# Spacing the side products of a fused attention kernel: halved projections, a rule against neighbouring units, and zero-valued products at the start

## The chip, the cores and the metric

One core of a Trainium2 chip runs the program. The metric is the device time of one execution in microseconds (us); the time of a kernel is the median of its runs.

## The reference, cut to what matters

Two layers over x of 4 x 1024 x 128 (float32), 16 heads of width 8, each sublayer followed by a residual sum and a layer norm without weights:

```
x = LN(x + attn0(x))   # q, k scaled to unit length, scores / temperature, full softmax, projection + bias
x = LN(x + ffn0(x))    # rows quantised to int8 with a scale of their own, int8 weights, one 128x128 product
x = LN(x + attn1(x))   # per-head layer norm of q and k, rotary embedding, causal softmax, projection + bias
x = LN(x + ffn1(x))    # down(silu(gate(x)) * up(x)), hidden width 384
```

Almost all of the work is attention: the exponential of every score (half of them in the causal layer), and two products of inner size 8 or of output width 8 for each score.

## The kernel before, in words

**Passes and slots.** The 4096 rows are 8 chunks of 512 (`CHUNKS`, line 48, gives the order in which the 16 pairs of layer and chunk are worked). A pass is one group of 4 heads of one chunk in one layer (64 passes, line 50); two passes share one accumulator bank. A step (line 89) is one tile of 128 keys against 512 queries for 4 heads; in the causal layer tiles are put together so that all steps have about the same width. There are 400 steps, and the program is a list of 400 slots, one for each step. In slot s TensorE issues the scores of the coming step as two groups k = 2s+3 and 2s+4 (`scores`, line 970: four products of 32 x 512 by two heads each), and the sums of step s-1 (`sums`, line 996: 8 products with the values, whose extra column of ones gives the softmax denominators). ScalarE takes two exponentials of 128 x 1024 for each step (line 826), 800 in all. Scores lie in three double banks of PSUM, so the scores of group k wait for the exponential of group k-3 (line 984). GpSimd cuts the causal corner out of the probabilities (line 734) and places the values (line 702).

**Units.** All other work is cut into units (lines 109 to 124): `qkv`, `qkT` (turns of q and k), `xqT`, `ffn`, `normT`, `gate`, `up`, `down` and `proj` on TensorE, each filling the one bank `SIDE` and read by VectorE before the next fill (`stage`, line 933; `read`, line 1358), and steps of layer norms, row norms and rotary embedding on VectorE. A job is the chain of units of one chunk: `prep` (before layer 0), `mid` (between the layers, through ffn0) and `last` (ffn1). The projection of a chunk, `proj`, isn't part of a job: it has a fixed slot, three behind the last step of the chunk's fourth pass (line 258), and is 16 calls of the product in four tiles of 128 rows (line 943), then one VectorE sum of 128 x 512 into `x_all` (line 1367).

**The planner.** `side_order` (line 176) writes down once, before the program is built, which units stand in which slot. Jobs are taken by their due slot; `after` is the first slot of a job. A table of costs (lines 146 to 152) keeps a running estimate of when TensorE, ScalarE and VectorE are free. In each slot at most one TensorE unit is placed (`done`), the first live job whose unit fits (`fits`, line 223); what VectorE units fit follow. Slots get one of three orders of TensorE's work: sums behind both score groups and ahead of the unit (the plain order), sums behind the unit (`front`), or sums between the two score groups (`between`, line 241). The list of the kernel before holds 202 TensorE units in 202 slots; 158 of them stand before slot 340, and the last 60 slots hold 44. Nothing in it keeps a unit from standing in the slot behind another unit's.

**Queues.** SP's queue carries the loads of q and k rows (`load_rows`, line 574), the stores of their parts (`send_parts`, line 550) and the output, in the order of a list sorted by the planner's slots (line 640).

**The start.** Before the first scores TensorE turns q and k of the first two chunks. `keep_warm` (line 1043) issues products of a tile of zeros, `warm`, whose result is overwritten later; `WARM` (line 522) counts them at four places. `FIRST_KEYS` (line 170) are three units of the second chunk that stand in slots 0 and 1: the turn of k in slot 0, and in slot 1 the scaling of q (VectorE) and the turn of q.

**The end.** Behind slot 400 `end` (lines 888 and 1301) runs the projection and ffn1 of the last chunk, one step after another.

Of the kernel before, what the change touches and what calls it, by code (L numbers as in the profile page):

```python
# [145 lines left out]
PE_US = {"qkT": 0.6, "normT": 0.6, "qkv": 0.9, "proj": 1.15, "xqT": 0.4, "ffn": 0.4, "gate": 0.7, "up": 0.7, "down": 0.95}  # L146
READ_US = {"qkT": 1.5, "normT": 0.65, "qkv": 0.6, "proj": 0.75, "xqT": 0.45, "ffn": 1.2, "gate": 0.75, "up": 1.5, "down": 0.35}
# [28 lines left out]
def side_order():  # L176
# [10 lines left out]
    for c in range(NCH):  # L187
        after = LAST_STEP[passes_of(0, c)[-1]] + 4
        jobs.append(dict(name="mid", c=c, after=after, due=min(first_slot(passes_of(1, c)[0]) - 4, after + 28)))
    for c in range(NCH - 1):  # L190
        after = LAST_STEP[passes_of(1, c)[-1]] + 4
        jobs.append(dict(name="last", c=c, after=after, due=min(after + 26, NS - 6)))
# [6 lines left out]
    out[1] += FIRST_KEYS[1:]  # L199
    turns = [LAST_STEP[p] + 1 for p in range(1, NP, 2)]  # L200
    pe = act = dve = bank = turned = 0.0
    scores_at = [0.0, 0.0]
    for s in range(NS + 1):
# [31 lines left out]
        project = [p for p in range(1, NP, 2) if PASSES[p][3] == GB - 1 and LAST_STEP[p] + 3 == s]  # L235
        if pending or not ends_pair(s - 1) and s <= NS - FREE and (
                dve < pe - 0.1 if project else any(fits(j, pe - AHEAD) for j in live)):
            front.add(s)
        else:
            one = max(free, act - act_time(s) / 2 if s < NS else 0.0) + 0.45 + cost  # L240
            if s < NS - 1 and max(one, act) + 0.45 < sums - GAIN:
                between.add(s)
                sums = one
                pe = max(one, act) + 0.45
                scores_at[-1] = pe + 0.05
            else:
                pe = sums
        done = False
        late = []
        for p in range(1, NP, 2):  # L250
            layer, b, qh, g = PASSES[p]
            if LAST_STEP[p] + 1 == s:
                out[s].append((None, p, "dve", "turn", p))
# [4 lines left out]
            if g == GB - 1 and LAST_STEP[p] + 3 == s:  # L258
                out[s].append((None, p, "pe", "proj", p))
                pe = max(pe, bank) + PE_US["proj"]  # L260
                dve = bank = max(dve, pe + 0.15) + READ_US["proj"]
                done = True
        for j in live:
# [4 lines left out]
            if not fits(j, pe + (SLACK if s < NS - END else LATE)):  # L268
                continue
# [30 lines left out]
SLACK, LATE, OVER, TURN_BY, END, FREE, AHEAD, GAIN = 0.2, 1.5, 1.6, 1.6, 60, 3, 0.0, -0.2  # L300
# [89 lines left out]
def program(nc, a, ctx):  # L390
# [131 lines left out]
    WARM = (10, 4, 0, 22)  # L522
# [340 lines left out]
    def _(pe):  # L863
# [69 lines left out]
        def stage(name, c, what, k):  # L933
# [4 lines left out]
            if what == "proj":  # L938
                layer, b, qh, g = PASSES[k]
                if k == GB - 1:  # L940
                    pe.wait_ge(late_consts, 1)
                pe.wait_ge(attn_ready, k // GB + 1)
                for t in range(TC):
# [124 lines left out]
        def steps(shifted):  # L1068
# [10 lines left out]
            for s in range(NS + 1):  # L1079
                for k in (2 * s + 3, 2 * s + 4):  # L1080
                    if k < 2 * NS:
                        scores(k, shifted)
                    if k % 2 and s in BETWEEN:
                        sums(s - 1)
                if s and s not in FRONT and s not in BETWEEN:
                    sums(s - 1)
# [15 lines left out]
    def _(dve):  # L1102
# [255 lines left out]
        def read(name, c, what, k):  # L1358
# [4 lines left out]
            if what == "proj":  # L1363
                layer, b, qh, g = PASSES[k]
                dve.wait_ge(bias_added, k // GB + 1)
                x = x_all[:, b * NH2 + qh, :, :]
                tt(x, side_t, x, ALU.add).then_inc(side_read, 1)  # L1367
# [176 lines left out]
```

## Time and profile before

| what | value |
|---|---|
| median of 3 runs | 831.9 us (831.88 to 832.3) |
| the profiled execution, its own time | 833.45 us |
| its span, first to last instruction | 831.4 us |
| mean granted TensorE clock | 0.993 of full speed |
| VectorE busy | 540.3 us (65%) |
| GpSimd busy | 169.9 us (20%) |
| first exponential starts | 20.24 us |
| last exponential starts | 805.6 us |

How to read it: the span is 2.05 us shorter than the execution's own time, and that execution is 1.55 us above the median. The stretch from the first to the last exponential is the 400 slots; 20 us before it are the head, 25 us behind it the end. Busy time of TensorE counts matmuls from issue to a modelled end, and these overlap, so it says when TensorE had work in flight and not how much more it could take.

### The profile page before, as it was taken

How to read it: one execution, taken by the hardware profiler on the slowest of the kernel's cores; microseconds unless marked ns; L12 is line 12 of the kernel's file. 1: busy time of each engine (PE TensorE's matmuls, PEld its weight loads, DVE VectorE, ACT ScalarE, POOL GpSimd, SP SyncE). 2: the span in 40 equal slices, each digit the busy share in tenths (PEclk: the TensorE clock that was granted, in tenths of full speed). 3: DMA queues.
4: the chain of work that ended last, by engine and by line, in shares of the span. 5: the costliest groups of instructions: out<-in, count | busy, mean ns of one | idle time of the engine just before them, and what ended most of it. 6: DMA issues, size and time to landing. Idle time of an engine off the chain costs nothing.

```text
span 831.4 us, 18912 instructions
## 1 busy us (share of the span) xinstructions
PE 803.6 (97%) x7457; PEld 295.6 (36%) x7457; DVE 540.3 (65%) x1426; ACT 772.3 (93%) x869; POOL 169.9 (20%) x370
## 2 busy tenths in 40 slices
PE   8899999999999999999999999999999999999996
PEld 4223332333333433343333433343333343443444
DVE  4265666868867787876663677675754267785656
ACT  4899999999999999999999999999999999898972
POOL 3110000100000601033000611023200354362220
PEclk9899999999999999999999999999999999999999
DMA  5765414242602631362130421321231231071000
GB/s 144 248 225 190 177 40 146 83 141 76 242 27 88 231 140 39 99 232 78 59 133 26 150 81 39 140 90 45 72 130 51 81 110 51 27 240 53 15 14 15
DMA packets 48556, 88.74 MB, mean 107 GB/s; under 512 B 5200, under 2 KB 14544, under 8 KB 48464
## 3 DMA queue, kind: packets, MB, share of 16 engines
q1 hardware_dynamic: 47696, 85.95, 30.4%
q8 instruction: 61, 1.00, 0.5%
q0 software_dynamic: 288, 1.05, 0.4%
q10 hardware_dynamic: 480, 0.48, 0.2%
q14 instruction: 31, 0.25, 0.1%
HBM read 50.50 MB, written 35.65 MB: 104 GB/s over the span
## 4 chain that ended last, share of the span: by engine, by line
PE 75%; ACT 13%; DVE 7%; issue 3%; DMA 0%; ACTq 0%; DVEq 0%
PE ps L1011 37%; PE ps L989 21%; ACT probs L826 13%; PE ps L879 9%; PE ps L868 3%; PE ps L964 3%; DVE th L1421 1%; DVE hT L1422 1%; PE ps L873 1%; PE ps L1045 1%; PE ps L1053 0%; DVE sums_t L1249 0%; DVE gate_sb L1416 0%; DVE mid_part L1411 0%; DVE mid_part L1412 0%
## 5 line engine op out<-in xcount | busy, mean ns | idle before, releaser
L826 ACT ACTIVATE probs<-ps 128x1024 f32<-128x1024 f32 x800 | 749.3, 1057 | 31.0 <-PE ps L989 21.2
L1011 PE MATMUL ps<-probs,v_st 128*32 128x512 f32 (+3 forms) x3584 | 428.1, 560 | 3.2 <-issue 2.4
L989 PE MATMUL ps<-q_st,k_st 32*128 32x512 f32 (+3 forms) x1792 | 266.3, 460 | 7.8 <-ACT probs L826 7.2
L989 PEld LDWEIGHTS ps<-q_st,k_st 32*128 32x128 f32 x1792 | 120.1, 182 | 288.0 <-ACT probs L826 221.7
L734 POOL TENSOR_SCALAR_AFFINE_SELECT probs<-probs 128x256 f32<-128x256 f32 x256 | 103.8, 428 | 144.7 <-ACT probs L826 143.0
L1011 PEld LDWEIGHTS ps<-probs,v_st 128*32 128x32 f32 x3584 | 78.7, 108 | 110.4 <-issue 74.2
L702 POOL COPY v_st<-v_all 128x256 f32<-128x256 f32 (+1 forms) x65 | 29.1, 456 | 343.2 <-PE ps L1011 334.9
L1249 DVE STREAM_TRANSPOSE sums_t<-ps 128x512 f32<-128x512 f32 x32 | 22.9, 716 | 45.3 <-PE ps L1011 44.7
L1390 DVE COPY mid_qkv<-ps 128x384 f32<-128x384 f32 x32 | 17.8, 557 | 35.8 <-PE ps L879 34.8
L964 PE MATMUL ps<-yTp,w_hid 128*128 128x512 f32 x84 | 31.2, 453 | 4.1 <-DVE gate_sb L1416 2.5
L1390 DVE COPY prep_qkv<-ps 128x384 f32<-128x384 f32 x24 | 13.4, 558 | 27.1 <-PE ps L879 26.4
L879 PE MATMUL ps<-w_cols,yT 128*32 128x384 f32 x256 | 26.7, 489 | 0.0
L1426 DVE TENSOR_TENSOR last_y<-ps,last_y 128x128 f32<-128x128 f32 x24 | 7.0, 292 | 28.8 <-PE ps L879 28.4
L1421 DVE SCALAR_TENSOR_TENSOR th<-th,gate_sb 128x512 f32<-128x512 f32 x21 | 14.8, 707 | 16.6 <-PE ps L964 16.2
L879 PE MATMUL ps<-w_down,hT 128*32 128x128 f32 x672 | 23.8, 275 | 1.1 <-DVE last_y L1426 0.6
L724 POOL TENSOR_TENSOR x_all<-x_all,vecs 128x512 f32<-128x512 f32 x16 | 23.3, 1459 | 1.1 <-DMA x_all<-in_x 1.1
L1367 DVE TENSOR_TENSOR x_all<-ps,x_all 128x512 f32<-128x512 f32 x15 | 10.4, 691 | 20.3 <-PE ps L879 12.4
L964 PEld LDWEIGHTS ps<-yTp,w_hid 128*128 128x128 f32 x84 | 12.6, 189 | 29.5 <-issue 9.3
L1416 DVE COPY gate_sb<-ps 128x512 f32<-128x512 f32 x21 | 14.5, 692 | 12.7 <-PE ps L964 12.4
L879 PEld LDWEIGHTS ps<-w_down,hT 128*32 128x32 f32 x672 | 17.9, 110 | 13.2 <-issue 7.4
L697 POOL COPY v_all<-prep_qkv 128x512 f32<-128x512 f32 x6 | 3.7, 614 | 85.7 <-DVEq L1393 85.7
L879 PE MATMUL ps<-w_cols,xT 128*32 128x384 f32 x192 | 20.1, 490 | 0.4 <-DVE hT L1422 0.2
(190 smaller groups left out, 641.3 us busy)
## 6 DMA issues: line engine op xcount, KB each, us to landing
k_st<-parts_scratch SPq DMA_DIRECT2D x46, 512.0 KB, 3.6
parts_scratch<-mid_part SPq DMA_DIRECT2D x34, 512.0 KB, 4.4
q_st<-parts_scratch SPq DMA_DIRECT2D x62, 256.0 KB, 3.9
parts_scratch<-prep_part SPq DMA_DIRECT2D x28, 512.0 KB, 4.8
k_st<-parts_scratch SPq DMA_DIRECT2D x17, 256.0 KB, 2.9
xT<-in_xT SPq DMA_DIRECT2D x8, 256.0 KB, 4.4
x_all<-in_x SPq DMA_DIRECT2D x8, 256.0 KB, 5.3
out<-yo SPq DMA_DIRECT2D x7, 256.0 KB, 2.3
```

The costliest lines, as they stand in the source:

```text
L702: return g_.tensor_copy(v_st[:, p % VB, t, :, p % 2 * SR:p % 2 * SR + D], v_all[:, layer, b % 2, t, g * GH * D:(g + 1) * GH * D] .rearrang ...
L724: g_.tensor_tensor(x_all[:, c, :, :], x_all[:, c, :, :], bc(vecs[:, 3 * layer, :].unsqueeze(1), [P, TC, C]), ALU.add).then_inc(bias_added, 1)
L734: op = g_.affine_select(out=block_, in_=block_, compare_op=ALU.is_ge, fill=0.0, base=0, pattern=[[0, 2], [1, P]], channel_multiplier=-1)
L826: nc.scalar.activation(probs[:, k % PS, :, 0:w], slot(k)[:, :, 0:w], ACT.Exp).then_inc(probs_ready, 1)
L868: last_ = tp(dst[:, t * P:(t + 1) * P], src(t), idn[:])
L879: last_ = mm(dst[row, :], src[:, row], w, start=first, stop=last)
L964: last_ = mm(side, w_hid[:, 0 if what == "gate" else 1, k * P:(k + 1) * P], yTp[:, n, :], start=(n == 0), stop=(n == PARTS - 1))
L989: last_ = mm(slot(k)[:, e, at:at + n], k_st[row, p % KB, kt * P:(kt + 1) * P], q_st[row, p % KB, lo:HALF], start=True, stop=not shifted)
L1011: last_ = mm(acc[HR * h:HR * (h + 1), lo:HALF], v_st[:, p % VB, kt, h, :], probs[:, (2 * s + h // 2) % PS, h % 2, at:at + n], start=FIRST[ ...
L1249: v.transpose(sums_t[:], acc).then_inc(sums_turned, 1)
L1390: v.tensor_copy(job[name]["qkv"][:, k, :], side[:, 0:3 * C]).then_inc(side_read, 1)
L1421: chain[lane(name, c)].link(stt(out=th[:, k % 2, :], in0=th[:, k % 2, :], scalar=1.0, in1=gate_sb[:, k % 2, :], op0=ALU.add, op1=ALU.mult))
```

## The change

- The projection of a chunk becomes two units of two tiles each, in the third and in the fourth slot behind the chunk, each with a VectorE sum of 128 x 256. The jobs that follow it start one slot later (`+ 5` for `+ 4`), and the table of costs has the new sizes.
- Up to slot 340 a TensorE unit is not placed when the slot before it holds one, as long as the job still reaches its due slot by the estimate `slots_left`: one slot for each TensorE unit left and 0.6 for each VectorE unit left.
- In slots 0 and 1, behind each of the score groups 3 to 6, two products of the zero tile go into the accumulator bank (which the first sums overwrite).
- The turn of q of the second chunk moves from slot 1 to slot 2, and the order with sums between the score groups is used only from slot 7 on.

```
@@ -143,8 +143,8 @@
 
 
 
-PE_US = {"qkT": 0.6, "normT": 0.6, "qkv": 0.9, "proj": 1.15, "xqT": 0.4, "ffn": 0.4, "gate": 0.7, "up": 0.7, "down": 0.95}
-READ_US = {"qkT": 1.5, "normT": 0.65, "qkv": 0.6, "proj": 0.75, "xqT": 0.45, "ffn": 1.2, "gate": 0.75, "up": 1.5, "down": 0.35}
+PE_US = {"qkT": 0.6, "normT": 0.6, "qkv": 0.9, "proj": 0.5, "xqT": 0.4, "ffn": 0.4, "gate": 0.7, "up": 0.7, "down": 0.95}
+READ_US = {"qkT": 1.5, "normT": 0.65, "qkv": 0.6, "proj": 0.45, "xqT": 0.45, "ffn": 1.2, "gate": 0.75, "up": 1.5, "down": 0.35}
 DVE_US = {"ln_stats": 0.9, "ln_aggr": 0.8, "ln_out": 1.2, "ln_out_x": 1.2, "ln_out_y": 1.2, "amax": 1.2, "quant": 1.0,
           "round": 1.0, "ffn_bias": 0.75, "add": 0.75, "square": 1.7, "norms": 1.3, "scale": 1.3,
           "rope0": 1.3, "rope1": 1.5, "rope2": 1.3, "rope3": 1.3, "weights": 2.8, "centre": 1.5, "rot": 2.0,
@@ -185,10 +185,10 @@
         after = first_slot(passes_of(0, c // NH2 * NH2 - NH2 - 1)[-1]) + 3 if c >= 2 * NH2 else BRANCHED
         jobs.append(dict(name="prep", c=c, after=after, due=first_slot(passes_of(0, c // NH2 * NH2)[0]) - 4))
     for c in range(NCH):
-        after = LAST_STEP[passes_of(0, c)[-1]] + 4
+        after = LAST_STEP[passes_of(0, c)[-1]] + 5
         jobs.append(dict(name="mid", c=c, after=after, due=min(first_slot(passes_of(1, c)[0]) - 4, after + 28)))
     for c in range(NCH - 1):
-        after = LAST_STEP[passes_of(1, c)[-1]] + 4
+        after = LAST_STEP[passes_of(1, c)[-1]] + 5
         jobs.append(dict(name="last", c=c, after=after, due=min(after + 26, NS - 6)))
     jobs.append(dict(name="consts", c=0, after=BRANCHED, due=16))
     for j in jobs:
@@ -196,8 +196,14 @@
     jobs.sort(key=lambda j: (j["due"], j["c"]))
     out, front, between = [[] for _ in range(NS + 1)], set(), set()
     out[0] += FIRST_KEYS[:1]
-    out[1] += FIRST_KEYS[1:]
+    out[1] += FIRST_KEYS[1:2]
+    out[2] += FIRST_KEYS[2:]
     turns = [LAST_STEP[p] + 1 for p in range(1, NP, 2)]
+
+    def slots_left(j):
+
+        return sum(REST if e == "pe" else 0.6 for e, what, k in UNITS[j["name"]][j["n"]:])
+
     pe = act = dve = bank = turned = 0.0
     scores_at = [0.0, 0.0]
     for s in range(NS + 1):
@@ -232,13 +238,13 @@
                     return False
             return True
 
-        project = [p for p in range(1, NP, 2) if PASSES[p][3] == GB - 1 and LAST_STEP[p] + 3 == s]
+        project = [p for p in range(1, NP, 2) if PASSES[p][3] == GB - 1 and 0 <= s - LAST_STEP[p] - 3 < 2]
         if pending or not ends_pair(s - 1) and s <= NS - FREE and (
                 dve < pe - 0.1 if project else any(fits(j, pe - AHEAD) for j in live)):
             front.add(s)
         else:
             one = max(free, act - act_time(s) / 2 if s < NS else 0.0) + 0.45 + cost
-            if s < NS - 1 and max(one, act) + 0.45 < sums - GAIN:
+            if BRANCHED <= s < NS - 1 and max(one, act) + 0.45 < sums - GAIN:
                 between.add(s)
                 sums = one
                 pe = max(one, act) + 0.45
@@ -255,8 +261,8 @@
                 turned = dve - 0.9
                 if g == GB - 1 and p < NP - 1:
                     late.append((None, p, "dve", "yT", p))
-            if g == GB - 1 and LAST_STEP[p] + 3 == s:
-                out[s].append((None, p, "pe", "proj", p))
+            if g == GB - 1 and 0 <= s - LAST_STEP[p] - 3 < 2:
+                out[s].append((None, p, "pe", "proj", s - LAST_STEP[p] - 3))
                 pe = max(pe, bank) + PE_US["proj"]
                 dve = bank = max(dve, pe + 0.15) + READ_US["proj"]
                 done = True
@@ -266,6 +272,8 @@
             name, c = j["name"], j["c"]
             e, what, k = UNITS[name][j["n"]]
             if not fits(j, pe + (SLACK if s < NS - END else LATE)):
+                continue
+            if s < NS - END and any(x[2] == "pe" for x in out[s - 1]) and s + slots_left(j) < j["due"]:
                 continue
             out[s].append((name, c, e, what, k))
             j["n"] += 1
@@ -297,7 +305,7 @@
 
 
 
-SLACK, LATE, OVER, TURN_BY, END, FREE, AHEAD, GAIN = 0.2, 1.5, 1.6, 1.6, 60, 3, 0.0, -0.2
+SLACK, LATE, OVER, TURN_BY, END, FREE, AHEAD, GAIN, REST = 0.2, 1.5, 1.6, 1.6, 60, 3, 0.0, -0.2, 1.0
 SIDE_ORDER, JOBS, FRONT, BETWEEN = side_order()
 
 LEFT = [(j["name"], j["c"], *u) for j in JOBS for u in j["left"]]
@@ -519,7 +527,7 @@
     shift_out, shift_in = sem("shift_out"), sem("shift_in")
 
     POOL_CONSTS = 11
-    WARM = (10, 4, 0, 22)
+    WARM = (10, 4, 0, 22, 7)
     NLATE = 9
     layer_job = ("prep", "mid")
     buffers = lambda name, c: job["mid" if (name, c) == ("prep", 1) else name]
@@ -936,11 +944,11 @@
             if fill:
                 pe.wait_ge(side_read, fill)
             if what == "proj":
-                layer, b, qh, g = PASSES[k]
-                if k == GB - 1:
+                layer, b, qh, g = PASSES[c]
+                if c == GB - 1:
                     pe.wait_ge(late_consts, 1)
-                pe.wait_ge(attn_ready, k // GB + 1)
-                for t in range(TC):
+                pe.wait_ge(attn_ready, c // GB + 1)
+                for t in range(2 * k, 2 * k + 2):
                     last_ = quarters(side[:, t * P:(t + 1) * P], attn[:, t * P:(t + 1) * P], w_out[:, layer, :])
             elif what == "normT":
                 pe.wait_ge(norm_ready[lane(name, c)], norm_number(name, c))
@@ -1082,6 +1090,8 @@
                         scores(k, shifted)
                     if k % 2 and s in BETWEEN:
                         sums(s - 1)
+                    if k < WARM[4]:
+                        keep_warm(2, ACC)
                 if s and s not in FRONT and s not in BETWEEN:
                     sums(s - 1)
                 for name, c, e, what, k in SIDE_ORDER[s]:
@@ -1361,10 +1371,10 @@
             got = lambda: dve.wait_ge(side_read, fill + 1)
             dve.wait_ge(side_filled, fill + 1)
             if what == "proj":
-                layer, b, qh, g = PASSES[k]
-                dve.wait_ge(bias_added, k // GB + 1)
-                x = x_all[:, b * NH2 + qh, :, :]
-                tt(x, side_t, x, ALU.add).then_inc(side_read, 1)
+                layer, b, qh, g = PASSES[c]
+                dve.wait_ge(bias_added, c // GB + 1)
+                x = x_all[:, b * NH2 + qh, tiles(k), :]
+                tt(x, side_t[:, tiles(k), :], x, ALU.add).then_inc(side_read, 1)
                 got()
             elif what == "normT" and name == "last":
                 ch = chain[lane(name, c)]
```

## Rows read from the trace of the kernel before

**Rows 1.** Page, part 1: busy time, share of the span, instructions

```profile
PE 803.6 (97%) x7457; PEld 295.6 (36%) x7457; DVE 540.3 (65%) x1426; ACT 772.3 (93%) x869; POOL 169.9 (20%) x370
```

**Rows 2.** Page, part 5, exponentials: busy, mean ns, idle before them and its releaser

```profile
L826 ACT ACTIVATE probs<-ps 128x1024 f32<-128x1024 f32 x800 | 749.3, 1057 | 31.0 <-PE ps L989 21.2
```

**Rows 3.** Timeline of ScalarE: start, duration, group, count, idle before it

```profile
20.24 6.52 ACT L826 ACTIVATE probs<-ps 128x1024 f32<-128x1024 f32 x7 [3.98 <-PE ps L989]
28.53 1.02 ACT L826 ACTIVATE probs<-ps 128x1024 f32<-128x1024 f32 x1 [1.77 <-PE ps L989]
30.95 110.32 ACT L826 ACTIVATE probs<-ps 128x1024 f32<-128x1024 f32 x117 [1.40 <-PE ps L989]
...
757.69 1.02 ACT L826 ACTIVATE probs<-ps 128x1024 f32<-128x1024 f32 x1 [2.16 <-PE ps L989]
```

**Rows 4.** Timeline of ScalarE in three windows: dense units, alternating units, no units

```profile
304.07 13.43 ACT L826 ACTIVATE probs<-ps 128x1024 f32<-128x1024 f32 x13
...
601.62 13.90 ACT L826 ACTIVATE probs<-ps 128x1024 f32<-128x1024 f32 x15 [0.36 <-PE ps L989]
...
639.00 21.19 ACT L826 ACTIVATE probs<-ps 128x1024 f32<-128x1024 f32 x23 [0.16 <-PE ps L989]
```

**Rows 5.** Timeline of TensorE around a whole projection (L879 with w_out)

```profile
89.53 0.59 PE L989 MATMUL ps<-q_st,k_st 32*128 32x512 f32 x4
90.05 1.06 PE L1011 MATMUL ps<-probs,v_st 128*32 128x512 f32 x8
90.93 1.06 PE L879 MATMUL ps<-w_out,attn 128*32 128x128 f32 x32
91.92 0.51 PE L989 MATMUL ps<-q_st,k_st 32*128 32x512 f32 x4
...
93.35 0.68 PE L989 MATMUL ps<-q_st,k_st 32*128 32x512 f32 x4
```

**Rows 6.** Timeline of VectorE: sums of a whole and of a half projection

```profile
92.06 0.69 DVE L1367 TENSOR_TENSOR x_all<-ps,x_all 128x512 f32<-128x512 f32 x1 [2.03 <-PE ps L879]
...
811.20 0.42 DVE L1308 TENSOR_TENSOR x_all<-ps,x_all 128x256 f32<-128x256 f32 x1 [0.61 <-PE ps L896]
```

**Rows 7.** Timeline of TensorE at the start, and one turn later (60.81)

```profile
1.27 4.45 PE L1045 MATMUL ps<-warm 128*128 128x512 bf16 x10 [1.27 <-DVE warm L1110]
...
14.27 4.91 PE L1045 MATMUL ps<-warm 128*128 128x512 bf16 x22
...
24.07 0.79 PE L989 MATMUL ps<-q_st,k_st 32*128 32x512 f32 x2 [0.42 <-ACT probs L826]
24.79 1.94 PE L1011 MATMUL ps<-probs,v_st 128*32 128x512 f32 x8
26.65 1.12 PE L868 MATMUL ps<-ident,mid_qk 128*128 128x128 f32 x4
...
60.81 0.66 PE L868 MATMUL ps<-ident,prep_qk 128*128 128x128 f32 x4
```

**Rows 8.** Table by stretch: length; busy PE, PEld, DVE, ACT, POOL; granted clock, DMA share, GB/s

```profile
22.00:23.00 1.00, 0.50 (x2) 0.18 (x2) 0.85 (x2) 1.00 (x3) 0.16 (x1) 1.00 0.38 90
...
24.00:25.00 1.00, 0.94 (x6) 0.48 (x10) 0.00 (x0) 1.00 (x3) 1.00 (x5) 0.50 0.84 315
...
31.00:32.00 1.00, 1.00 (x10) 0.18 (x2) 0.00 (x0) 1.00 (x2) 0.00 (x0) 1.00 1.01 377
...
754.00:757.50 3.50, 3.50 (x14) 0.86 (x14) 1.41 (x2) 1.54 (x2) 0.54 (x2) 0.51 0.02 5
```

**Rows 9.** Timeline of SP, a load of q for pass 2; page, part 6, such loads

```profile
40.68 0.43 SPq L572 DMA_DIRECT2D q_st<-parts_scratch  x1
...
q_st<-parts_scratch SPq DMA_DIRECT2D x62, 256.0 KB, 3.9
```

**Rows 10.** Timeline of TensorE in slot 375 and of VectorE behind slot 397

```profile
753.96 1.13 PE L964 MATMUL ps<-yTp,w_hid 128*128 128x512 f32 x2 [1.31 <-DVE gate_sb L1416]
...
806.96 1.12 DVE L1188 TENSOR_SCALAR yo<-mid_y,mid_tok 128x128 f32<-128x128 f32 x4
```

More of the change, by code:

```diff
@@ L142, in ends_pair @@
     return STEPS[s][5] and STEPS[s][0] % 2 == 1
-PE_US = {"qkT": 0.6, "normT": 0.6, "qkv": 0.9, "proj": 1.15, "xqT": 0.4, "ffn": 0.4, "gate": 0.7, "up": 0.7, "down": 0.95}
-READ_US = {"qkT": 1.5, "normT": 0.65, "qkv": 0.6, "proj": 0.75, "xqT": 0.45, "ffn": 1.2, "gate": 0.75, "up": 1.5, "down": 0.35}
+PE_US = {"qkT": 0.6, "normT": 0.6, "qkv": 0.9, "proj": 0.5, "xqT": 0.4, "ffn": 0.4, "gate": 0.7, "up": 0.7, "down": 0.95}
+READ_US = {"qkT": 1.5, "normT": 0.65, "qkv": 0.6, "proj": 0.45, "xqT": 0.45, "ffn": 1.2, "gate": 0.75, "up": 1.5, "down": 0.35}
 DVE_US = {"ln_stats": 0.9, "ln_aggr": 0.8, "ln_out": 1.2, "ln_out_x": 1.2, "ln_out_y": 1.2, "amax": 1.2, "quant": 1.0,
@@ L198, in side_order, with slots_left @@
     out[0] += FIRST_KEYS[:1]
-    out[1] += FIRST_KEYS[1:]
+    out[1] += FIRST_KEYS[1:2]
+    out[2] += FIRST_KEYS[2:]
     turns = [LAST_STEP[p] + 1 for p in range(1, NP, 2)]
+    def slots_left(j):
+        return sum(REST if e == "pe" else 0.6 for e, what, k in UNITS[j["name"]][j["n"]:])
     pe = act = dve = bank = turned = 0.0
@@ L233, in fits @@
             return True
-        project = [p for p in range(1, NP, 2) if PASSES[p][3] == GB - 1 and LAST_STEP[p] + 3 == s]
+        project = [p for p in range(1, NP, 2) if PASSES[p][3] == GB - 1 and 0 <= s - LAST_STEP[p] - 3 < 2]
         if pending or not ends_pair(s - 1) and s <= NS - FREE and (
@@ L240, in side_order @@
             one = max(free, act - act_time(s) / 2 if s < NS else 0.0) + 0.45 + cost
-            if s < NS - 1 and max(one, act) + 0.45 < sums - GAIN:
+            if BRANCHED <= s < NS - 1 and max(one, act) + 0.45 < sums - GAIN:
                 between.add(s)
@@ L257, in side_order @@
                     late.append((None, p, "dve", "yT", p))
-            if g == GB - 1 and LAST_STEP[p] + 3 == s:
-                out[s].append((None, p, "pe", "proj", p))
+            if g == GB - 1 and 0 <= s - LAST_STEP[p] - 3 < 2:
+                out[s].append((None, p, "pe", "proj", s - LAST_STEP[p] - 3))
                 pe = max(pe, bank) + PE_US["proj"]
@@ L268, in side_order @@
             if not fits(j, pe + (SLACK if s < NS - END else LATE)):
+                continue
+            if s < NS - END and any(x[2] == "pe" for x in out[s - 1]) and s + slots_left(j) < j["due"]:
                 continue
@@ L521, in program @@
     POOL_CONSTS = 11
[L522 removed]
+    WARM = (10, 4, 0, 22, 7)
     NLATE = 9
@@ L938, in stage @@
             if what == "proj":
-                layer, b, qh, g = PASSES[k]
-                if k == GB - 1:
+                layer, b, qh, g = PASSES[c]
+                if c == GB - 1:
                     pe.wait_ge(late_consts, 1)
-                pe.wait_ge(attn_ready, k // GB + 1)
-                for t in range(TC):
+                pe.wait_ge(attn_ready, c // GB + 1)
+                for t in range(2 * k, 2 * k + 2):
                     last_ = quarters(side[:, t * P:(t + 1) * P], attn[:, t * P:(t + 1) * P], w_out[:, layer, :])
@@ L1363, in read @@
             if what == "proj":
[L1364 to L1367, printed above, removed]
+                layer, b, qh, g = PASSES[c]
+                dve.wait_ge(bias_added, c // GB + 1)
+                x = x_all[:, b * NH2 + qh, tiles(k), :]
+                tt(x, side_t[:, tiles(k), :], x, ALU.add).then_inc(side_read, 1)
                 got()
```

8 lines of the change are left out of this document (5 added, 3 removed).

## The prediction

> **What bounds the kernel now.** I read the page's busy shares first. TensorE is at 97%, ScalarE at 93% [rows 1], so either could be the bound, and the share is a mean over stages. The exponentials decide: 800 of them, with 31.0 us of idle time ahead of them, most of it waiting for scores [rows 2]. ScalarE's timeline gives their pace. Where slots hold no unit, 23 exponentials take 21.19 us, and since the last one is seen for 1.02 us that is (21.19 - 1.02)/22 = 0.917 us each, 1.83 us for a slot [rows 4]; I take this as ScalarE's own pace. Where every slot holds a unit, it is (13.43 - 1.02)/12 = 1.034, or 2.07 us for a slot [rows 4]. So ScalarE is the bound where units are rare and TensorE where they stand in a row, 0.24 us worse for each slot. The third row is the one to remember: units at slots 300, 302, 304, 306 and 307, and the exponentials still come every (13.90 - 1.02)/14 = 0.920 us [rows 4]. A unit with an empty slot behind it costs almost nothing, because TensorE needs only 93.35 - 91.92 = 1.43 us for an empty slot [rows 5], 0.40 less than ScalarE, and catches up.
>
> All 800 at 0.917 us would take 734 us; the first start and the last lie 785 us apart. The 21 tanh that ScalarE also runs are a small part of the 51 us between; the rest is lost, and three things in this change reach for it.
>
> **1. The start.** Seven exponentials run on time, then ScalarE waits 1.77 and 1.40 us [rows 3]: 3.17 us in all. Ahead of that TensorE was busy for half of the stretch from 22 to 23 us, and from 24 us the granted clock is 0.50, that is 1.2 GHz, until it is back at 1.00 from 31 us [rows 8]. The first sums take 1.94 us and the turn of q 1.12 [rows 7], where at full clock the same work takes 1.06 [rows 5] and 0.66 [rows 7]. The change fills the gaps between the score groups 3 to 6 with pairs of zero products. Do such products hold the clock? The first ten took 4.45/10 = 0.445 us each, the later 22 only 4.91/22 = 0.223 [rows 7], so zero-valued products run at the full rate, with nothing else in between. A pair takes 0.45 us and the gaps are 0.42 [rows 7], covered by the exponentials, of which there are always two ahead. With the clock held, group 6 issues at 24.07, its pair ends at 24.95, the sums at 26.0, and group 7 is done by 26.5; the eighth exponential is due at 20.24 + 7 x 0.917 = 26.66, so no wait. The turn of q, now in slot 2, then sits between the sums of step 1 and group 9: 26.5 + 0.5 + 1.06 + 0.66 = 28.7, against 28.5 due. I take 3.17 - 0.2 = **-2.9 us**. Bounds: -3.17, and +1.7 if the clock falls all the same and half of the eight products (0.445 each at the low clock) lie on the path.
>
> What could be late next: everything at the start is wanted 3 us earlier. The tightest are the q rows of pass 2, issued at 40.68 and landing 3.9 us later, at 44.6 [rows 9]; group 32 would then be issued at about 20.24 + 29 x 0.917 = 46.8. Two microseconds remain. The stores that these loads wait for stand behind others in SP's queue and not behind the turn of q, which by the sum above ends no later than before.
>
> **2. The halved projections.** A whole one makes its slot 91.92 - 89.53 = 2.39 us long on TensorE [rows 5], 0.56 over ScalarE's pace. Half adds 0.48 to the empty 1.43: 1.91, 0.08 over. Twice 0.08 for 0.56 would save 0.40; if each half cost as much as a unit in a row (0.24), it would save 0.08. Slack of the empty slots around already absorbs some of the 0.56, so I take 0.25, for 15 projections **-3.75 us** (bounds -6.0 and -1.2). VectorE reads two halves of 0.42 for one of 0.69 [rows 6]; it is 65% busy [rows 1], and its next readers wait for TensorE. Starting the jobs one slot later costs nothing up to slot 340: the rows of a `mid` chunk are first needed tens of slots behind its due slot.
>
> **3. The spaced units.** From the planner's list of the kernel before I count 94 units before slot 340 that stand directly behind another: 35 second in a run, 59 further back. At 0.24 us for those further back, and half of it for the second (which the slack of the slot before partly pays), that is 59 x 0.24 + 35 x 0.12 = 18.4 us. How many remain? Between the slots 7, 57, 132, 232 and 340 there were 20, 39, 52 and 45 units in 50, 75, 100 and 108 slots; with the second halves 21, 42, 56 and 49. The two middle stretches hold more than every second slot can take, and u units in n slots leave at least 2u - n - 1 neighbours: 8 and 11. Jobs close to their due slot may also run on. A `mid` job has 28 slots and an estimate of 9 + 0.6 x 24 = 23.4, so it can afford about 5 of its 6 gaps; a `last` job has 26 for 17; `prep` has room throughout. I guess 40 neighbours, 30 of them second: 30 x 0.12 + 10 x 0.24 = 6.0 us, and 1.0 us more for the many new lone units. **18.4 - 7.0 = -11.4 us** (bounds: -16 with only the 19 that must remain, 0 if the rule seldom bites).
>
> **4. The last 60 slots.** The rule is off there; the jobs start one slot later. In slot 375 a gate waited 1.31 us for VectorE [rows 10], the clock went to 0.51 at 754 us [rows 8], and ScalarE lost 2.16 us [rows 3]. A plan shifted by a slot may miss this (-3) or meet it elsewhere; VectorE's last piece of the seventh chunk, 1.12 us at 806.96 [rows 10], may slide into the closing chain (+2). I take 0.
>
> **Sum:** -2.9 - 3.75 - 11.4 + 0 = -18.0. The profiled execution took 833.45, so it would be 815.4; the median of the runs is 1.55 lower, and 831.9 - 18.0 = **813.9, say 814 us**.
>
> **The rivals.**
> - **The clock falls at the start anyway.** The zero products come only from group 3 on, and the turn of k lies in the same stretch. Then part 1 is between 0 and +1.7: 814 + 2.9 + 1 = **818**. For it: one fall there is on record; against it: the 22 at full rate. The Trainium skill ("TensorE: Matmul & The Clock Gate", Part 4) says that a transpose does not count as activity as a matmul does; by that rule the moved turn of q would help the clock nowhere, and the time would be this rival's. No row here shows what a turn alone does to the clock.
> - **TensorE is full.** If 97% [rows 1] meant that it has nothing to give, order would not matter and only the start would gain: 831.9 - 2.9 = **829**. Against it: the alternating stretch [rows 4]. The Trainium skill ("Trainium Kernel Development and Optimization", Best Practices) warns against judging TensorE by matmul busy time and points to the share of weight loading; that is 36% here [rows 1], which leaves room, and the trace's 1.43 us agrees.
> - **Crowding, slower.** Put-off units gather before their due slots, where three jobs run at once (slots 132 to 232), and the halves take 15 more slots. Parts 1 and 2 give 6.65 us, which 6.65/0.24 = 28 more neighbours would eat: from 122 of them on (94 before) the change loses. With 150 it would be 831.9 - 6.65 + 56 x 0.24 = **839**. For it: the rule puts off without looking at what else falls due; against it: due slots are staggered and the count of units hardly grows.
> - **All of it.** 19 neighbours, full gain of the halves, and no fall of the clock at 754: 831.9 - 2.9 - 6 - 13 - 3 = **807**.
>
> **How the numbers follow.** The forecast (809 to 820) has 0.52, the fallen clock 0.17, all of it 0.12, a full TensorE 0.09, crowding 0.08, something late at the start or the end 0.02. The range must leave out no more than 0.2: from 806 (all of it) to 826 (the fallen clock with a smaller part 3), leaving out a full TensorE and crowding. A difference of 0.2%, 1.7 us, is about what a measurement of this kernel can tell. Faster by more has the first four cases, less a little for a full TensorE with nothing gained at the start: 0.88; the same 0.04; slower 0.08.
>
> **What would show it.** Right: a granted clock of 1.00 from 22 to 31 us, sums of 1.06 us there, and exponentials in one row from 20.24 on; slots with half a projection at about 1.9 us; the idle time ahead of the exponentials down from 31.0 to under 20 us; the stretch from 289 to 330 us, dense now, at less than 2 us a slot. Wrong: a row of 0.50 in the clock before 31 us; the dense pace of 1.034 over as many exponentials as now; idle exponentials waiting for DMA near 47 us, or the last one later than 800 us.

## The result, and the profile after

The change takes 827.48 us, median of three runs (826.92 to 827.58), against 831.9: ratio 0.9937, 95% interval 0.9922 to 0.9952. By the medians that is 4.4 us faster where 18 were forecast, 1.5 us above the range. The profiled execution took 827.58 us, with a span of 825.4 (831.4 before).

The page of the kernel after, part 1 (as [rows 1]), and from part 5 the exponentials (as [rows 2]) and the projections:

```profile
PE 793.8 (96%) x7457; PEld 294.5 (36%) x7457; DVE 539.2 (65%) x1437; ACT 770.9 (93%) x873; POOL 172.4 (21%) x370
...
L834 ACT ACTIVATE probs<-ps 128x1024 f32<-128x1024 f32 x800 | 747.1, 1058 | 27.2 <-PE ps L997 22.0
...
L887 PE MATMUL ps<-w_out,attn 128*32 128x128 f32 x480 | 18.8, 274 | 5.0 <-DVE attn L1266 5.0
```

The same group of projections in the kernel before, from its groups of TensorE by shape:

```profile
L879 PE MATMUL ps<-w_out,attn 128*32 128x128 f32 x480 | 16.0, 274 | 0.0
```

The busy shares hardly move. The idle time ahead of the exponentials falls from 31.0 to 27.2 us, of which the start alone should have given 3. And TensorE now waits 5.0 us ahead of the projections, for VectorE's `attn`; before, that group waited for nothing.

**The start** did what it should. Timeline of TensorE (as [rows 7]), then of ScalarE (as [rows 3]), then the table by stretch (as [rows 8]), all of the kernel after:

```profile
21.44 0.60 PE L1053 MATMUL ps<-warm 128*128 128x512 bf16 x2
...
24.87 1.07 PE L1019 MATMUL ps<-probs,v_st 128*32 128x512 f32 x8
...
27.30 0.66 PE L876 MATMUL ps<-ident,mid_qk 128*128 128x128 f32 x4
```

```profile
19.93 126.43 ACT L834 ACTIVATE probs<-ps 128x1024 f32<-128x1024 f32 x137 [4.01 <-PE ps L997]
```

```profile
22.00:23.00 1.00, 1.00 (x7) 0.33 (x6) 0.85 (x2) 1.00 (x2) 0.46 (x1) 1.00 0.42 115
24.00:25.00 1.00, 1.00 (x8) 0.33 (x12) 0.00 (x0) 1.00 (x2) 1.00 (x6) 1.00 0.99 365
28.00:29.00 1.00, 1.00 (x12) 0.23 (x12) 0.96 (x2) 0.93 (x2) 0.00 (x0) 1.00 0.73 260
```

The granted clock stays at 1.00 (2.4 GHz), the first sums take 1.07 us and the turn of q 0.66, and 137 exponentials run in one row where 7 did.

**The slots.** To compare the rest I took the starts of all 800 exponentials from the trace and computed how much longer than 1.81 us each slot is (the median slot without a unit takes 1.807), with 0.52 taken out for each tanh. A unit in slot s shows at the exponentials of step s+2. Over slots 4 to 337, count, mean and sum in us (the last column is an experiment told below):

| the slot holds | before | after | early turn |
|---|---|---|---|
| a projection, whole or half | 12, 0.405, 4.9 | 24, 0.238, 5.7 | 24, 0.019, 0.5 |
| no unit | 179, 0.012, 2.1 | 167, 0.007, 1.2 | 167, 0.007, 1.2 |
| a unit, none in the slot ahead | 49, 0.072, 3.5 | 91, 0.108, 9.9 | 91, 0.112, 10.2 |
| the second unit in a row | 35, 0.164, 5.7 | 20, 0.163, 3.3 | 20, 0.162, 3.2 |
| one further back in a row | 59, 0.257, 15.1 | 32, 0.238, 7.6 | 32, 0.235, 7.5 |

The neighbours give back 10.0 us, and the lone units (those with none in the slot ahead), of which there are now 91, take 6.4 of it. The projections, halved, cost more than whole.

The same count, parted by the kind of unit, shows part of why a lone unit now costs more on average. Without the five dearest, which are told of further below, the lone `ffn` and `xqT` of the kernel after cost 0.00 us (8 of them), the turns of q and k 0.06 (20), `qkv` 0.10 (31). In a row, `ffn` and `xqT` still cost 0.00 and `qkv` 0.27. TensorE works 0.85 us on a `qkv`, 0.66 on a turn and 0.40 on an `xqT`. Of the 42 new lone units 28 are `qkv`.

Why they do is seen at one of them. Timeline of all engines of the kernel after, slots 96 to 98 (start, duration, what ran, the idle time before it and its releaser):

```profile
202.70 0.72 DVE L1259 STREAM_TRANSPOSE sums_t<-ps 128x512 f32<-128x512 f32 x1 [0.53 <-PE ps L1019]
...
203.84 0.43 DVE L1263 TENSOR_TENSOR heads_t<-sums_t,rd 128x256 f32<-128x256 f32 x1
204.30 0.56 DVE L1400 COPY prep_qkv<-ps 128x384 f32<-128x384 f32 x1
...
204.77 1.22 DVE L1250 TENSOR_TENSOR mid_qk<-mid_qk,rot 128x1024 f32<-128x1024 f32 x1
...
206.13 0.71 DVE L1266 STREAM_TRANSPOSE attn<-heads_t 128x512 f32<-128x512 f32 x1
...
206.99 0.64 PE L887 MATMUL ps<-w_out,attn 128*32 128x128 f32 x16 [0.74 <-DVE attn L1266]
...
208.10 2.90 ACT L834 ACTIVATE probs<-ps 128x1024 f32<-128x1024 f32 x3 [0.66 <-PE ps L997]
```

Read it down VectorE. The chunk's sums are turned and divided by 204.27; the next step, the turn into `attn`, takes 0.71 us. But the planner lists it (`yT`) at the end of the slot, behind that slot's units: a copy of `qkv` and a rotary step run first, 1.8 us. TensorE reaches the first half projection, finds no `attn`, and stands 0.74 us; ScalarE then stands 0.66. By the planner's lists, 8 of the 13 chunk ends before slot 340 have a unit or a piece between `turn` and `yT` after the change, 4 before it: the rule puts units off into those slots. Waits of TensorE in the kernel after (in total, how many, the longest):

```profile
PE ps L887 <- DVE attn L1266: 5.0, 7, 1.2
...
PE ps L887 <- DVE hT L1432: 1.4, 2, 1.1
PE ps L876 <- DVEq L1305: 1.4, 1, 1.4
...
PE ps L876 <- DVE mid_qkv L1400: 1.2, 1, 1.2
```

**The end.** Slots 340 to 399 cost 15.7 us over pace, 16.5 before. But from the end of the last exponential to the end of the span it is 26.7 us, 24.7 before. The planner now leaves two `down` units and five VectorE pieces of the seventh chunk behind slot 400. Timelines of TensorE, VectorE and ScalarE at the end of the kernel after:

```profile
803.69 1.52 PE L887 MATMUL ps<-w_down,hT 128*32 128x128 f32 x48
```

```profile
815.23 0.16 DVE L383 TENSOR_SCALAR mid_tok<-mid_tok 128x4 int32<-128x4 int32 x1
...
816.80 0.16 DVE L1324 SCALAR_TENSOR_TENSOR mid_tok<-mid_tok 128x4 f32<-128x4 f32 x1
816.91 0.42 DVE L1352 TENSOR_TENSOR last_y<-ps,last_y 128x256 f32<-128x256 f32 x1
...
822.03 0.60 DVE L1362 TENSOR_SCALAR yo<-last_y,last_tok 128x128 f32<-128x128 f32 x2 [0.94 <-DMA out<-yo]
```

```profile
817.00 1.65 ACT L860 ACTIVATE yo<-mid_y,mid_tok 128x128 f32<-128x128 f32 x4 [4.37 <-DVE mid_tok L1324]
```

Nine small VectorE operations for the seventh chunk's norm stand from 815.23 to 816.96 just ahead of the sum that closes the last chunk, and near the end VectorE waits 0.94 us for a store.

**The account:** start -3.3 us, slots 4 to 339 -3.5, slots 340 to 399 -0.8, end +2.0, first exponential 0.3 earlier: -5.9, and the spans differ by 6.0. (The first exponential lies anywhere from 19.2 to 20.5 us in the profiles of this study; differences of single profiles are good to about a microsecond for that alone. The profiled execution of before was also 1.55 above its median, so that by medians 4.4 are left.)

### The profile page after: what moved, and what is told of

It reads as the page before. It is cut to its first block, busy times and chain, and to the rows that moved or that the text cites. A ratio compares the mean times of both kernels' runs of the same rounds, so it can differ in the third digit from the quotient of the medians.

```text
span 825.4 us, 18983 instructions
## 1 busy us (share of the span) xinstructions
PE 793.8 (96%) x7457; PEld 294.5 (36%) x7457; DVE 539.2 (65%) x1437; ACT 770.9 (93%) x873; POOL 172.4 (21%) x370
## 4 chain that ended last, share of the span: by engine, by line
PE 65%; DVE 15%; ACT 13%; issue 5%; DMA 1%; ACTq 0%; DVEq 0%
PE ps L1019 32%; PE ps L997 18%; ACT probs L834 13%; PE ps L887 7%; PE ps L972 3%; PE ps L876 3%; DVE th L1431 1%; DVE sums_t L1259 1%; DVE hT L1432 1%; DVE mid_y L1220 1%; PE ps L1053 1%; DVE attn L1266 1%; DVE heads_t L1263 1%; DVE mid_part L1421 1%; DVE mid_part L1422 1%
## 5 line engine op out<-in xcount | busy, mean ns | idle before, releaser
L834 ACT ACTIVATE probs<-ps 128x1024 f32<-128x1024 f32 x800 | 747.1, 1058 | 27.2 <-PE ps L997 22.0
L997 PE MATMUL ps<-q_st,k_st 32*128 32x512 f32 (+3 forms) x1792 | 258.2, 459 | 2.8 <-ACT probs L834 2.3
L742 POOL TENSOR_SCALAR_AFFINE_SELECT probs<-probs 128x256 f32<-128x256 f32 x256 | 106.0, 436 | 143.3 <-ACT probs L834 141.8
L710 POOL COPY v_st<-v_all 128x256 f32<-128x256 f32 (+1 forms) x65 | 31.0, 485 | 327.7 <-PE ps L1019 319.7
L1377 DVE TENSOR_TENSOR x_all<-ps,x_all 128x256 f32<-128x256 f32 x30 | 12.7, 425 | 27.9 <-PE ps L887 27.4
L887 PE MATMUL ps<-w_cols,yT 128*32 128x384 f32 x256 | 26.9, 491 | 0.4 <-DVE mid_qkv L1400 0.4
L705 POOL COPY v_all<-mid_qkv 128x512 f32<-128x512 f32 x9 | 5.5, 612 | 97.1 <-DVEq L1403 92.0
L887 PE MATMUL ps<-w_out,attn 128*32 128x128 f32 x480 | 18.8, 274 | 5.0 <-DVE attn L1266 5.0
```

The source lines that it names most:

```text
L710: return g_.tensor_copy(v_st[:, p % VB, t, :, p % 2 * SR:p % 2 * SR + D], v_all[:, layer, b % 2, t, g * GH * D:(g + 1) * GH * D] .rearrang ...
L742: op = g_.affine_select(out=block_, in_=block_, compare_op=ALU.is_ge, fill=0.0, base=0, pattern=[[0, 2], [1, P]], channel_multiplier=-1)
L834: nc.scalar.activation(probs[:, k % PS, :, 0:w], slot(k)[:, :, 0:w], ACT.Exp).then_inc(probs_ready, 1)
L887: last_ = mm(dst[row, :], src[:, row], w, start=first, stop=last)
L997: last_ = mm(slot(k)[:, e, at:at + n], k_st[row, p % KB, kt * P:(kt + 1) * P], q_st[row, p % KB, lo:HALF], start=True, stop=not shifted)
```

## The experiments

Each was timed against the kernel before on the same chip. The short names: the **rule** is the one against neighbours, **early turn** is the edit that lists `yT` early. In the texts on record e2 is the change without the rule, e3 early turn and e10 the run with 44 slots.

### The start part alone, on the kernel before

```
-    out[1] += FIRST_KEYS[1:]
+    out[1] += FIRST_KEYS[1:2]
+    out[2] += FIRST_KEYS[2:]
...
-            if s < NS - 1 and max(one, act) + 0.45 < sums - GAIN:
+            if BRANCHED <= s < NS - 1 and max(one, act) + 0.45 < sums - GAIN:
...
+                    if k < WARM[4]:
+                        keep_warm(2, ACC)
```

> The kernel before with the start of the change alone (zero products behind score groups 3 to 6, turn of q in slot 2, no sums between the groups ahead of slot 7). Theory A (the clock kept at 1.00 gives back the 3.2 us of waits): 831.9 - 3.2 = 828.7, between 828 and 829.5, and the idle time ahead of the exponentials down by 3. Theory B (the start only moves the waits to the loads behind it): 831 to 832. Under A the rule and the halves together gave only about 1 us of the 4.4.

Measured 829.52 us, ratio 0.9961 (0.9947 to 0.9976): 2.5 us. Slots 0 to 3 lose 0.17 us in place of 3.47; slots 4 to 339 lose 31.7, for 31.4 before. The start part is worth about what it was forecast at, and the halves, the rule and the end together only some 2 us. A second fall of the clock shows in this kernel too. TensorE waits for `gate` twice, at 702 and at 752 us (1.2 and 1.3 us), as in the kernel before. In the profile of this run the clock falls to 0.50 behind the first wait, in that of the kernel before behind the second [rows 8]; the slot behind the wait loses 2.2 or 2.3 us with the fall and 0.7 without it, so the fall costs 1.5.

### The change without the zero-valued products, and with the turn of q back in slot 1

```
-                    if k < WARM[4]:
-                        keep_warm(2, ACC)
```

> The changed kernel without the zero products in the first two slots; all else stays. Theory A (they keep the clock, and the clock was the start's whole loss): a granted clock of 0.50 from about 24 us again, sums of 1.94 us, waits of 2 to 3 us ahead of the eighth and later exponentials, 827.5 + 2.5 = 830, between 829.5 and 831. Theory B (moving the turn of q out of slot 1 already avoids the waits): 827 to 828.

```
-    out[1] += FIRST_KEYS[1:2]
-    out[2] += FIRST_KEYS[2:]
+    out[1] += FIRST_KEYS[1:]
```

> The changed kernel with the turn of q back in slot 1; zero products stay. Theory A (at full clock the turn costs at most a few tenths wherever it stands): 827.5 to 828. Theory B (the turn in slot 1 waits for VectorE and holds the scores up): 828.5 to 829.5, with a wait of over 0.5 us ahead of the eighth exponential.

Without the products 829.11 us (0.9961, 0.9947 to 0.9974), 1.6 above the whole change and a little under the range of A; with the turn in slot 1 828.23 (0.995, 0.9935 to 0.9966), 0.75 above, between the two ranges. Both intervals overlap the change's own, so the clock and the profiles have to decide. The mean granted clock is 0.992 in all five executions without the products, and 0.997 to 0.998 in those of the change and with the turn in slot 1 (one at 0.996). Table by stretch and ScalarE's timeline without the products, then ScalarE's timeline with the turn in slot 1:

```profile
22.00:23.00 1.00, 0.50 (x2) 0.18 (x2) 0.85 (x2) 1.00 (x2) 0.01 (x1) 1.00 0.36 90
24.00:25.00 1.00, 0.79 (x6) 0.36 (x10) 0.00 (x0) 1.00 (x3) 1.00 (x5) 0.50 0.68 258
28.00:29.00 1.00, 1.00 (x8) 0.00 (x0) 0.00 (x0) 1.00 (x2) 0.00 (x0) 0.50 0.63 193
```

```profile
27.64 1.94 ACT L834 ACTIVATE probs<-ps 128x1024 f32<-128x1024 f32 x2 [0.73 <-PE ps L997]
31.09 9.27 ACT L834 ACTIVATE probs<-ps 128x1024 f32<-128x1024 f32 x10 [1.52 <-PE ps L997]
```

```profile
26.37 13.87 ACT L833 ACTIVATE probs<-ps 128x1024 f32<-128x1024 f32 x15 [0.54 <-PE ps L996]
```

Without the products the clock falls to 0.50 again and two waits come back, 2.25 us; they sit where [rows 3] had them. With the turn in slot 1 and the products kept there is one wait of 0.54 and no fall. So the products hold the clock, and the moved turn saves about half a microsecond of TensorE's time at a tight place.

### The change without the rule

```
-            if s < NS - END and any(x[2] == "pe" for x in out[s - 1]) and s + slots_left(j) < j["due"]:
-                continue
```

> The changed kernel without the rule against neighbouring units; halves and start stay. By the planner's list the neighbours before slot 340 rise from 64 to 107. Theory A (each neighbour costs 0.2 us, the rule pays for itself): 827.5 + 43 x 0.2 = 836, less some waits for VectorE at chunk ends, so 832 to 836. Theory B (what the rule saves in neighbours it loses in waits for late VectorE pieces and in costs of lone units): 826 to 829.

Measured 831.69 us (0.9996, 0.9987 to 1.0005), just under the range of A: the rule is worth 4.2 us in the change, and the halves with the later jobs, on top of the start, cost 2.2. Half projections cost 0.094 us a slot here, 2.3 in all for 4.9 when whole, but the second halves make 107 neighbours out of 94, the rows further back cost 17.3 us for 15.1, and the end part is 26.9 us. TensorE waits for `attn` 1.9 us, for 5.0 with the rule: that wait needs the rule to grow.

```profile
PE ps L885 <- DVE attn L1264: 1.9, 3, 0.7
```

### Early turn: the same plan, with `yT` listed directly behind `turn`

```
+    for items in out:
+        for x in [x for x in items if x[3] == "yT"]:
+            items.remove(x)
+            items.insert([y[3] for y in items].index("turn") + 1, x)
```

> The changed kernel with the same plan, except that in the slot behind a chunk the turn of the heads (yT) is listed directly behind the turn of the sums, ahead of the units that the rule pushed into that slot. Theory A (the first half of the projection waits 5.0 us in all for this turn, because put-off units stand ahead of it): those waits fall under 1 us, and the time falls by 4 to 5, to 822.5 to 824. Theory B (the waits only move to the reads that now come later): 826.5 to 827.5.

Measured 822.27 us, ratio 0.988 (0.9863 to 0.9896), 5.2 us below the change: the interval lies wholly under the change's. All units stand in the same slots; only VectorE's order within nine of them differs. The same place as above, in the timeline of this kernel:

```profile
203.86 0.42 DVE L1267 TENSOR_TENSOR heads_t<-sums_t,rd 128x256 f32<-128x256 f32 x1
204.32 0.71 DVE L1270 STREAM_TRANSPOSE attn<-heads_t 128x512 f32<-128x512 f32 x1
...
204.95 0.52 DVE L1404 COPY prep_qkv<-ps 128x384 f32<-128x384 f32 x1
...
205.40 1.21 DVE L1254 TENSOR_TENSOR mid_qk<-mid_qk,rot 128x1024 f32<-128x1024 f32 x1
...
206.09 0.62 PE L891 MATMUL ps<-w_out,attn 128*32 128x128 f32 x16
```

The turn comes first, the half projection starts with no wait, 0.9 us earlier, and the copy and the rotary step lose nothing that shows. The waits for `attn` are gone from the list, half projections cost 0.019 us a slot (the table above), and the page has the exponentials at

```profile
L838 ACT ACTIVATE probs<-ps 128x1024 f32<-128x1024 f32 x800 | 746.1, 1064 | 22.8 <-PE ps L1001 18.0
```

This shows the cause of the projections' missing gain.

### Early turn without the rule

The second and the third edit together.

> Run e3 (early turn of the heads, 822.3) without the rule against neighbouring units: neighbours before slot 340 rise from 64 to 107, projections no longer wait. Theory A (a neighbour costs 0.22 and a lone unit 0.11, so the rule is worth about 7 us once the turn is early): 829 to 830.5. Theory B (the rule is worth 4 us whatever stands at the chunk ends, as between e2 and the changed kernel): 826 to 827.

Measured 830.42 us (0.9976, 0.9965 to 0.9986). With the turn early the rule is worth 830.42 - 822.27 = 8.1 us, with the turn late 4.2: some 4 us of what the rule gains were spent at the chunk ends.

### Whole projections, with the rule and the start part

The projection becomes one unit again in its third slot, and the jobs start at `+ 4`; in short

```
-            if g == GB - 1 and 0 <= s - LAST_STEP[p] - 3 < 2:
-                out[s].append((None, p, "pe", "proj", s - LAST_STEP[p] - 3))
+            if g == GB - 1 and (s - LAST_STEP[p] - 3 == 0 or s - LAST_STEP[p] - 3 == 1 and LAST_STEP[p] < 0):
+                half = LAST_STEP[p] < 0
+                out[s].append((None, p, "pe", "proj", s - LAST_STEP[p] - 3 if half else 2))
...
-                for t in range(2 * k, 2 * k + 2):
+                for t in range(4) if k == 2 else range(2 * k, 2 * k + 2):
```

> The changed kernel with whole projections again in the third slot behind a chunk and jobs from the fourth (costs of the table as before); rule and start stay. Neighbours before slot 340 fall to 48, nothing is left for the end. Theory A (halving gave 0.4 for each projection only where the turn was early, and cost neighbours and 1.8 us at the end): 825 to 828. Theory B (halving is worth the 3.75 us of the prediction): 830 to 832.

Measured 827.68 us (0.9948, 0.9934 to 0.9963): the same as the change. As it stands, halving is worth nothing. A whole projection costs 0.595 us here (7.1 in all, with two waits for `attn`), nothing is left behind slot 400, and the end part is back at 24.7 us. Halving gains in the slots (27.9 us over pace in slots 4 to 339, for 30.3 whole) what it loses at the end.

### Early turn, with whole projections and earlier jobs from slot 320 on

The same edit on early turn, with 320 in the place of 0, and `+ 4` for the chunks behind that slot alone.

> Run e3 (822.3) with whole projections and jobs one slot earlier from slot 320 on, so that the last slots hold the plan of the kernel before and nothing is left for the end. Theory A (halves in the full last slots push two down units and five VectorE pieces of the seventh chunk behind the last exponential, where they and the wait for its output lengthen the end from 24.8 to 27.6 us): the end is 24.8 us again, three whole projections cost about 1 us back, 820 to 821.5. Theory B (the end is set by the last chunk's own chain and only seems longer): 822.5 to 823.5.

Measured 822.13 us (0.9876, 0.9861 to 0.9892): no different from early turn. The end part fell as it should, from 27.5 to 24.7 us (the expectation has both 0.1 longer), and slots 340 to 399 took 1.7 of it back (15.4 to 17.1). In the list of TensorE's waits the one for `gate`, which the kernel before had too [rows 10] and early turn had not, is back:

```profile
PE ps L977 <- DVE gate_sb L1432: 3.1, 2, 1.9
```

Behind the longer of the two waits the granted clock is at 0.51 from 743.5 to 747 us.

### Early turn, with the sums ahead of the unit in nearly all slots

Is it the order within a slot that makes a lone unit cost 0.11 us?

```
+    for s in range(BRANCHED, NS - END):
+        if s in front and not (STEPS[s - 1][4] and STEPS[s - 1][0] % 2 == 0):
+            front.discard(s)
```

> Run e3 (822.3) with the same plan, but sums ahead of the unit (plain order) in all slots from 7 to 339 except where a pass begins; e3 had the unit ahead of the sums in most slots with a lone unit, and a lone unit cost 0.11 us there (91 of them, 10.2 us). Theory A (a lone unit costs that because TensorE can save up only about 0.2 us in an empty slot, in any order): 822 to 823. Theory B (the order holds the next scores up behind unit and sums): 3 to 5 us faster, 817.5 to 819.5.

Measured 824.53 us (0.9922, 0.9907 to 0.9937), 2.3 above early turn, slower than either theory had it, with lone units at 0.117. So it isn't that the unit stood ahead of the sums.

### Early turn, with later due slots: 44, 52, and 52 for the early jobs only

More room for the rule. The edit with 44 (42 for `last`), and that of the third of them (the second has 52 and 50 for every chunk), cut to the ends of the lines:

```
-due=min(first_slot(passes_of(1, c)[0]) - 4, after + 28)))
+due=min(first_slot(passes_of(1, c)[0]) - 4, after + 44)))
...
-due=min(first_slot(passes_of(1, c)[0]) - 4, after + 28)))
+due=min(first_slot(passes_of(1, c)[0]) - 4, after + (52 if c < 6 else 28))))
...
-due=min(after + 26, NS - 6)))
+due=min(after + (50 if c <= 3 else 26), NS - 6)))
```

> Run e3 (822.3) with later due slots for the jobs between and behind the layers (after + 44 for + 28, after + 42 for + 26), so that the rule can space more: neighbours before slot 340 fall from 64 to 42. Theory A (a neighbour made lone saves 0.22 - 0.11): 822.3 - 22 x 0.11 = 819.9, between 819 and 821. Theory B (put-off units meet late VectorE pieces and the waits eat it): 822 to 824. Theory C (the 0.23 of the prediction for each): 817.5.

> As run e10, with after + 52 and after + 50: neighbours fall to 30, of which 12 are the second halves of projections. Theory A: 822.3 - 34 x 0.11 = 818.6, between 817.5 and 819.5. Theory B: 822 to 825. Theory C: 814.5.

Measured 832.55 us (1.0008, 0.9999 to 1.0017) with 44, and 828.72 (0.9963, 0.9949 to 0.9976) with 52, both slower than any of the theories. One wait takes the gain away in both, 8.2 and 8.3 us. Waits of TensorE, ScalarE's timeline and the table by stretch with 52:

```profile
PE ps L1001 <- DMA q_st<-parts_scratch: 8.3, 1, 8.3
```

```profile
740.69 1.02 ACT L838 ACTIVATE probs<-ps 128x1024 f32<-128x1024 f32 x1 [7.54 <-PE ps L1001]
743.22 11.12 ACT L838 ACTIVATE probs<-ps 128x1024 f32<-128x1024 f32 x12 [1.50 <-PE ps L1001]
```

```profile
735.00:738.00 3.00, 0.00 (x0) 0.00 (x0) 0.13 (x1) 0.00 (x0) 0.00 (x0) 0.50 0.64 197
738.00:744.00 6.00, 4.20 (x30) 1.37 (x30) 0.00 (x0) 1.81 (x2) 0.40 (x1) 0.50 0.99 339
744.00:748.00 4.00, 3.65 (x48) 1.28 (x40) 1.72 (x4) 4.00 (x6) 1.33 (x4) 1.00 0.55 198
```

The last chunk's turns of q and k moved from slots 363 and 364 to 368 and 369, TensorE waited 8.3 us for the rows of q, and the clock stood at 0.50 around the hole. In slots 4 to 339, though, 34 fewer neighbours (30 for 64) saved 2.8 us, 20.0 for 22.8: 0.08 each. With 44 the 22 fewer saved only 0.6 us, 22.2 for 22.8: 0.03 each. Why so little isn't known. Hence the last run, which leaves the late jobs as they were:

> The early-turn kernel with the later due slots of the run before it, but only for jobs that end before slot 340: `mid` of chunks 0 to 5 due 52 slots behind its start, `last` of chunks 0 to 3 due 50 behind; `mid` of chunks 6 and 7 and the later `last` jobs keep the early-turn kernel's own due slots, so chunk 7's turns of q and k stand in slots 363 and 364 again instead of 368 and 369. Units behind a unit before slot 340: 39 (early turn 64, with all jobs late 30). Theory A: the 8.3 us wait for q_st was the whole harm of the late due slots, and a neighbour that gets room saves about 0.08 us: 25 x 0.08 = 2.0 us under the early-turn kernel's 822.3, so 820.3 us, slots 4 to 339 about 20.8 us over 1.81 each, no wait for q_st over 1 us. Theory B: VectorE's pieces pushed towards the end cost in the last 60 slots what the room saves: 822 to 824 us, slots 340 to 399 over 16.5 us.

Measured 820.72 us (819.3 to 821.57), ratio 0.9853 (0.9834 to 0.9873), the fastest kernel of the study, 11.8 us under the kernel before on that chip. Slots 4 to 339 cost 20.6 us (20.8 was expected), slots 340 to 399 15.8, and the wait for `q_st` is gone. Its interval overlaps that of early turn a little; the slots' 2.2 us agree with the difference. Its page has

```profile
L838 ACT ACTIVATE probs<-ps 128x1024 f32<-128x1024 f32 x800 | 745.1, 1052 | 21.0 <-PE ps L1001 17.7
```

and 123 units without a neighbour ahead still cost 13.9 us: that is what is left to find.

## Why the prediction was right, and where it was wrong

**Part by part.** Of 18.0 us forecast 5.9 came by the spans: the start -3.3 (-2.9 forecast), the halves +0.8 on the 12 projections before slot 340 (-3.75 on 15), the spacing -3.6 (-11.4), the last slots and the end +1.2 (0), and -1.0 in slots without a unit and ahead of the first exponential. The miss lies in the halves, 4.6 us, and in the spacing, 7.8.

**What bounds the kernel: right.** ScalarE where units are rare, TensorE where they stand in rows. The second unit in a row cost 0.164 us (0.12 taken), one further back 0.257 (0.24 taken).

**1. The start: right.** -2.9 forecast, -2.5 by the run of the start alone and -3.3 in the slots. No load was late behind it. The clock did not fall, so the first rival is out. The rule of the Trainium skill cited there ("TensorE: Matmul & The Clock Gate", Part 4, that a transpose does not count as activity as a matmul does) was not put to the test: with the products in place the clock stayed at 1.00 with the turn in either slot.

**2. The halves: the mechanism right, the step that failed is "its next readers wait for TensorE".** A projection gained 0.405 - 2 x 0.019 = 0.37 us when the turn was early (0.25 taken), but in the change the 12 before slot 340 lost 0.8 us together. A slot with a half, 1.91 us in the sum, took 2.05 in the change and 1.83 with the turn early. I costed VectorE's side by its busy share, 65%, and by the sums behind the projection, and never asked what it does ahead of it. An engine with a third of its time free still does its list in order, and 1.8 us of work with room to spare stood ahead of a 0.71 us turn with none. The early-turn run shows it. In the kernel before, the turn stood behind other work at 4 of these 13 places, and no projection waited: the waits came with the plan of the change.

**3. The spacing: the step that failed is the sum for what remains.** The gain on the neighbours was sized well for its count: 20.9 us before (18.4 taken) and 10.9 after. But 64 neighbours remained, 12 of them second halves, where I guessed 40; and the new lone units, which I gave 1.0 us, took 6.4. I had read "costs almost nothing" from one stretch of alternating units [rows 4], at 0.920 us per exponential, and carried it to all. The kernel before had 49 lone units already, at 0.072 us each, and its trace would have shown it ahead of the forecast. In the change a lone unit costs 0.108 us on average. Five of the 91 cost over 0.25 us, 3.2 us together, and four of these, 2.9 us, stand behind waits for VectorE; the other 86 cost 0.077 each. That cost goes with the kind of unit, and most of the new lone units are of the dear kind, `qkv`; why a `qkv` with an empty slot ahead still costs 0.10 us no run shows. A neighbour that is given room therefore saves not 0.24 but 0.08 or 0.09, by the run with 52 and the last run, and 0.03 by the run with 44. The guess of 40 fell because the due slots and not the rule set how many remain: with 52 slots for the job there are 30.

**4. The end: 0 taken, +2.0 measured, -0.8 in the last 60 slots.** The +2 was named, but for one VectorE piece that slides; it was two units and five pieces. With whole projections and the jobs one slot earlier nothing is left over, and the end part is 24.7 us; which of the two does it was not tried. The -3 was half there: both waits for `gate` (2.5 us) and the fall of the clock behind them (1.5) are gone, but other waits for VectorE, 1.4 us for `hT` and 1.2 for `mid_qkv` in the list above among them, took most of it back.

**The rivals.** A full TensorE gave 829 and the result lies near it, for another reason: early turn, with the same work on TensorE, ran 5.2 us faster. Crowding was half right: the rule does put off without looking at what else falls due, but the price was not more neighbours, it was VectorE's list at the chunk ends. The dense stretch became 33 exponentials in 31.55 us from 290.51 on, as the prediction's last section has it (under 2 us a slot); the idle time under 20 us did not come, even in the fastest kernel (21.0). One price among the rivals was wrong in itself: "all of it" counts 13 us for 19 neighbours where part 3 has 16, by which it would be 804 us and outside the range. Nothing measured came near either.

## What to carry to other kernels

When a planner is free to put work off, look where it lands: ask for each short step on the critical chain what now stands ahead of it in its own engine's list, and place such a step by what waits for it and not at the end of its slot. Price the spaced case from several stretches and by kind of work, not from the best one: here a gap gave back a third of what the crowded case cost. And when due times are loosened, exempt the last job of a chain, whose output a load waits for.

## What the runs showed of the hardware

Pairs of zero-valued bf16 products, 0.60 us a pair, kept TensorE's granted clock at 1.00 through a stretch in which it fell to 0.50 without them. Ahead of the fall TensorE was half busy (0.50 us from 22 to 23), and none of its gaps between the score groups was longer than 0.42 us [rows 7]. Without the products the two waits that return are 2.25 us, and the time is 1.6 us longer by the medians.
